# Storing two output tiles side by side in four strips, in a batched bilinear kernel on one Trainium2 core

## The reference

```python
bilinear = jnp.einsum('bie,ied->bid', feature, weight)   # feature (512, 200, 64), weight (200, 64, 64)
out = jnp.einsum('bid,bjd->bij', bilinear, feature)      # (512, 200, 200)
```

## Time and profile before

| | |
|---|---|
| median of 3 runs | 312.74 us (312.12 to 316.39) |
| profiled execution | 311.45 us |
| its span | 309.7 us |
| mean granted TensorE clock in it | 0.944 of 2.4 GHz |
| busy, share of the span: TensorE / DVE / ACT | 77% / 49% / 42% |
| TensorE's instructions | 6,784 matmuls and as many weight loads |
| DMA queue q1, share of the 16 engines' span | 91.0% |

### The profile page before, as it was taken

How to read it: one execution, slowest core, us unless ns; L and a number is a source line. 1 busy time by engine, 2 the same in 40 slices (tenths; PEclk the granted TensorE clock), 3 DMA queues, 4 the chain that set the end, 5 groups by cost and what they waited for, 6 DMA issues and landing times.

```text
span 309.7 us, 14622 instructions
## 1 busy us (share of the span) xinstructions
PE 239.8 (77%) x6784; PEld 209.1 (68%) x6784; DVE 152.7 (49%) x180; ACT 130.2 (42%) x181; POOL 12.5 (4%) x23
## 2 busy tenths in 40 slices
PE   0269757999867776899988597989975985999960
PEld 0257746878766665677977496867975975978840
DVE  0253543457654544537756443536653464736650
ACT  1343524346344433345555333344543453544530
POOL 2005700000000000000000000000000000000000
PEclk9996999899999979999999977999998799999995
DMA  7997999859999999968999999997899998577996
GB/s 259 402 421 302 366 395 380 349 218 365 359 400 404 408 414 409 413 245 351 336 415 396 412 418 413 414 392 276 336 354 400 384 418 360 229 310 295 400 410 287
DMA packets 26140, 112.35 MB, mean 363 GB/s; under 512 B 4320, under 2 KB 4320, under 8 KB 25824
## 3 DMA queue, kind: packets, MB, share of 16 engines
q1 hardware_dynamic: 26080, 111.43, 91.0%
HBM read 29.49 MB, written 81.92 MB: 360 GB/s over the span
## 4 chain that ended last, share of the span: by engine, by line
PE 77%; issue 14%; DMA 3%; SPq 1%; DVE 1%; ACT 1%
PE psum L292 50%; PE psum L263 18%; PE psum L309 8%; DMA w_sb<-w_dram 3%; SPq L152 1%; PE psum L275 1%; DVE tile L324 1%; ACT mixed L345 0%; ACT w_sb L359 0%
## 5 line engine op out<-in xcount | busy, mean ns | idle before, releaser
L292 PE MATMUL psum<-x_sb,mixed 64*64 64x200 f32 x3072 | 170.3, 354 | 27.8 <-issue 26.5
L292 PEld LDWEIGHTS psum<-x_sb,mixed 64*64 64x64 f32 x3072 | 134.3, 140 | 47.3 <-issue 35.0
L324 DVE COPY tile<-psum 128x800 f32<-128x800 f32 x100 | 99.2, 992 | 109.7 <-PE psum L292 99.2
L324 ACT COPY tile<-psum 128x800 f32<-128x800 f32 x100 | 82.5, 826 | 86.0 <-PE psum L292 69.4
L263 PE MATMUL psum<-x_sb,w_sb 64*64 64x64 f32 x3072 | 67.9, 230 | 29.9 <-issue 16.2
L263 PEld LDWEIGHTS psum<-x_sb,w_sb 64*64 64x64 f32 x3072 | 66.3, 143 | 31.0 <-issue 29.3
L345 ACT COPY mixed<-psum 64x512 f32<-64x512 f32 x48 | 27.8, 580 | 34.5 <-PE psum L263 33.9
L345 DVE COPY mixed<-psum 64x512 f32<-64x512 f32 x48 | 33.1, 689 | 10.7 <-PE psum L263 9.4
L347 ACT COPY mixed<-psum 128x512 f32<-128x512 f32 x24 | 14.1, 586 | 36.6 <-PE psum L263 36.6
L309 PE MATMUL psum<-x_sb,tails 128*32 128x200 f32 x512 | 25.3, 342 | 1.4 <-issue 1.4
L309 PEld LDWEIGHTS psum<-x_sb,tails 128*32 128x32 f32 x512 | 17.0, 108 | 8.9 <-issue 4.2
(11 more groups left out here) (3 smaller groups left out, 0.3 us busy)
## 6 DMA issues: line engine op xcount, KB each, us to landing
out_dram<-tile SPq DMA_DIRECT2D x192, 400.0 KB, 5.6
x_sb<-x_dram SPq DMA_DIRECT2D x64, 400.0 KB, 7.4
out_tail_dram<-tile SPq DMA_DIRECT2D x8, 400.0 KB, 3.6
w_sb<-w_dram SPq DMA_DIRECT2D x1, 1152.0 KB, 16.7
w_sb<-w_dram SPq DMA_DIRECT2D x4, 256.0 KB, 8.2
w_sb<-w_dram SPq DMA_DIRECT2D x1, 1024.0 KB, 14.5
```

The lines of the kernel that those rows point to most:

```text
L292: last = nc.tensor.matmul(psum[half_rows(pair), n % BANK_PAIRS * 2 + h, a * FIELDS:(a + 1) * FIELDS], mixed[half_rows(h), (CHUNKS * g + c) ...
L324: copy(tile[:, k % SLOTS, engine], psum[:, bank:bank + 2, 0:2 * FIELDS]).then_inc(copied[engine], 1)
```

## The change

Two tiles in sequence (k even, and k + 1) share one slot: they lie side by side in each partition, 12,800 bytes. There are three such slots, `tile` has the same size. SP waits for the copies of both tiles and then stores the pair in four strips, each of every fourth partition (32 packets of 12,800 bytes), and issues the loads that belong to either tile after these. The last pair is stored tile by tile in two strips each. The copies wait for the stores of the pair three places before. The output tensor holds pairs, and the tail's tiles are in it with the others; the host takes them apart.

```diff
--- before.py
+++ after.py
@@ -33,9 +33,11 @@
 
 LAST_WAITED = MIX_AFTER[(PART - CHUNK) // MIX_FIELDS]
 TAIL_AFTER = (2, 4)
-SLOTS = 6
-
-STRIPS = 2
+
+
+SIDE = 2
+SLOTS = 3
+STRIPS = 4
 STRIP_STORES = STRIPS * 16
 
 
@@ -120,9 +122,16 @@
 
 COPIES, READERS, NUMBER, OUT_TILES = count_copies()
 TILE_OF = {tile: k for k, tile in enumerate(OUT_TILES)}
-
-
-def build(nc, x, weight, out, out_tail):
+PAIRS = len(OUT_TILES) // SIDE
+
+
+def tile_copies(tile, e):
+
+    kind, g, *rest = tile
+    return COPIES[NUMBER[(kind, g, *rest, e)]][e]
+
+
+def build(nc, x, weight, out):
     sb = lambda name, shape: nc.alloc_sbuf_tensor(name, shape, F32)
 
     w_sb = sb("w_sb", [128, 2, W_OWN, EMB])
@@ -131,7 +140,7 @@
 
 
     tails = sb("tails", [128, QUADS, 2 * TAIL_TILE // (2 * TAIL), HALVES, TAIL])
-    tile = sb("tile", [128, SLOTS, 2, HALVES, 2 * FIELDS])
+    tile = sb("tile", [128, SLOTS, SIDE, 2, HALVES, 2 * FIELDS])
     psum = nc.alloc_psum_tensor("psum", [128, 2 * BANK_PAIRS, BANK], F32)
 
     sem = nc.alloc_semaphore
@@ -171,23 +180,34 @@
                 load_part1(sp, 0, p)
             for n in range(MIX_UNITS, len(W_CUTS) - 1):
                 load_w(n)
-            for k, (kind, g, *rest) in enumerate(OUT_TILES):
-                to = out_tail[g] if kind == "tail" else out[g, rest[0], rest[1]]
-                for e in range(2):
-                    n = NUMBER[("tail", g, e) if kind == "tail" else ("score", g, *rest, e)]
-                    sp.wait_ge(copied[e], COPIES[n][e])
-                for i in range(STRIPS):
-                    sp.dma_start(to[i::STRIPS], tile[i::STRIPS, k % SLOTS]).then_inc(slot_out[k % SLOTS], 16)
-                if kind == "score" and g + 1 < GROUPS:
-                    c, t = rest
-                    if c == 0:
-
-                        load_part0(sp, g + 1, t)
-                    if c == CHUNKS - 1:
-
-                        load_part1(sp, g + 1, t)
+            for pair in range(PAIRS):
+                tiles = OUT_TILES[pair * SIDE:(pair + 1) * SIDE]
+                if pair < PAIRS - 1:
+                    for e in range(2):
+                        sp.wait_ge(copied[e], max(tile_copies(tiles[0], e), tile_copies(tiles[1], e)))
+                    for i in range(STRIPS):
+                        sp.dma_start(out[pair, i::STRIPS], tile[i::STRIPS, pair % SLOTS]).then_inc(
+                            slot_out[pair % SLOTS], 16)
+                else:
+
+                    for side in range(SIDE):
+                        for e in range(2):
+                            sp.wait_ge(copied[e], tile_copies(tiles[side], e))
+                        for i in range(STRIPS // SIDE):
+                            strip = slice(i, None, STRIPS // SIDE)
+                            sp.dma_start(out[pair, strip, side], tile[strip, pair % SLOTS, side]).then_inc(
+                                slot_out[pair % SLOTS], 16)
+                for kind, g, *rest in tiles:
+                    if kind == "score" and g + 1 < GROUPS:
+                        c, t = rest
+                        if c == 0:
+
+                            load_part0(sp, g + 1, t)
+                        if c == CHUNKS - 1:
+
+                            load_part1(sp, g + 1, t)
             for s in range(SLOTS):
-                sp.wait_ge(slot_out[s], STRIP_STORES * len(range(s, len(OUT_TILES), SLOTS)))
+                sp.wait_ge(slot_out[s], STRIP_STORES * len(range(s, PAIRS, SLOTS)))
 
         @block.gpsimd
         def _(pool):
@@ -318,10 +338,11 @@
         def copies(eng, copy, engine):
 
             def copy_tile(n, k):
-                if k >= SLOTS:
-                    eng.wait_ge(slot_out[k % SLOTS], STRIP_STORES * (k // SLOTS))
+                pair, side = divmod(k, SIDE)
+                if pair >= SLOTS:
+                    eng.wait_ge(slot_out[pair % SLOTS], STRIP_STORES * (pair // SLOTS))
                 bank = n % BANK_PAIRS * 2
-                copy(tile[:, k % SLOTS, engine], psum[:, bank:bank + 2, 0:2 * FIELDS]).then_inc(copied[engine], 1)
+                copy(tile[:, pair % SLOTS, side, engine], psum[:, bank:bank + 2, 0:2 * FIELDS]).then_inc(copied[engine], 1)
 
             def score(n, g, c, t, u):
                 if u == engine:
@@ -387,17 +408,19 @@
     nc = bacc.Bacc("TRN2", target_bir_lowering=False, num_devices=1)
     args = [nc.dram_tensor("x_dram", x.shape, F32, kind="ExternalInput").ap(),
             nc.dram_tensor("w_dram", w.shape, F32, kind="ExternalInput").ap()]
-    shapes = {"out_dram": (GROUPS, CHUNKS, TILES, 128, 2, HALVES, 2 * FIELDS),
-              "out_tail_dram": (GROUPS, 128, 2, HALVES, 2 * FIELDS)}
-    args += [nc.dram_tensor(n, s, F32, kind="ExternalOutput").ap() for n, s in shapes.items()]
+    shape = (PAIRS, 128, SIDE, 2, HALVES, 2 * FIELDS)
+    args.append(nc.dram_tensor("out_dram", shape, F32, kind="ExternalOutput").ap())
     build(nc, *args)
     r = run_bass_kernel_spmd(nc, [{"x_dram": x, "w_dram": w}], core_ids=[0]).results[0]
 
-
-    rows = r["out_dram"].reshape(GROUPS, CHUNKS, TILES, 2, CHUNK, 2, HALVES, 2, FIELDS)
+    tiles = r["out_dram"].reshape(PAIRS, 128, SIDE, 2, HALVES, 2 * FIELDS).swapaxes(1, 2).reshape(
+        len(OUT_TILES), 128, 2, HALVES, 2 * FIELDS)
+    order = [TILE_OF["score", g, c, t] for g in range(GROUPS) for c in range(CHUNKS) for t in range(TILES)]
+
+    rows = tiles[order].reshape(GROUPS, CHUNKS, TILES, 2, CHUNK, 2, HALVES, 2, FIELDS)
     rows = rows.transpose(0, 6, 2, 5, 7, 3, 1, 4, 8).reshape(GROUPS, HALVES, HALF_SAMPLES, TAIL_FIRST, FIELDS)
 
-    tail = r["out_tail_dram"].reshape(GROUPS, 4, 2, HALVES, TAIL, 2, 2, 2, FIELDS)
+    tail = tiles[[TILE_OF["tail", g] for g in range(GROUPS)]].reshape(GROUPS, 4, 2, HALVES, TAIL, 2, 2, 2, FIELDS)
     tail = tail.transpose(0, 3, 5, 6, 7, 1, 2, 4, 8).reshape(GROUPS, HALVES, HALF_SAMPLES, TAIL, FIELDS)
     whole = np.concatenate([rows, tail], axis=3)
```

## The result

| | before | after |
|---|---|---|
| median | 313.03 us (312.12 to 316.39, 4 runs) | 317.12 us (316.74 to 317.93, 4 runs) |
| profiled execution's span | 309.7 us | 315.0 us |
| DMA packets on q1 | 26,080 | 19,808 |
| q1's share of 16 engines' span | 91.0% | 89.0% |

The ratio is 1.0136 (95% interval 1.0081 to 1.0191): slower by 1.4%, clear of noise. The forecast was 310.7 us, 2.0 us less than before, in a range of 305 to 317. The ratios here leave out executions that lie more than 1.5% above the fastest of the same kernel, so they may differ from the quotient of the medians, which are of all executions.

What follows compares the result with a forecast made beforehand. The prediction took DMA to bound the kernel in 195 us and TensorE in 81 us. Fewer packets saved 2.0 us, all other terms were zero: 312.74 - 2.0 = 310.7 us, range 305 to 317.

Steps and rivals of the forecast that it cites:

- bounds of 306.5 and 319 us: Limits used for the prediction's chances: 0.12 below 306.5 us, 0.80 within, 0.08 above 319 us.
- The bound: Whole span: DMA bounds the kernel in five stretches, 195 us, and TensorE in those between, 81 us.
- under 0.95: Sign of a wrong forecast: DMA share under 0.95 in 80:125 or 160:200, pointing to held tile or slots.
- the wait for `out_dram` at every other tile: Sign of a wrong forecast, pointing to the slots: ACT or DVE waiting for `out_dram` at every other tile.
- Fewer packets, -2.0 us: Stores in DMA-bound stretches: 70 tiles x 4 packets x 7 ns saved, 2.0 us; 0 to 6.2 us at the bounds.
- nothing: Rival for the stores: cost goes by bytes, or packets are cut on the way; 312.7 us, chance 0.17.
- Waiting for the second tile, 0: Five places where DMA goes from idle to busy, and DMA-bound stretches: the first tile's later store costs zero.
- comes out of that backlog: DMA-bound stretches: transfers lag the copies, so a hold of one tile (2 to 3 us) doesn't run DMA dry.
- The slots, 0: Three slots of two: five tiles take 10 us, copy to landing under 9.8 us, so it just fits; zero.
- Loads later, 0: Even tiles' loads issued one tile (3 us) later, needed well after: zero, bound 3 us once in a group.
- held tile: Rival: at five places DMA starts one store later, not absorbed, 8.7 us more; 321 us, chance 0.11.
- fetch: Rival: TensorE's instruction blocks wait 0.25 us more behind longer packets, 17 blocks, 4.2 us; 314.9 us, chance 0.06.

Runs made afterwards that it cites:

- hold_only: Kernel before with SP's new order alone (waits for both tiles, four stores, then their loads), six slots, 6,400-byte packets: 317.75 us, ratio 1.0116.
- hold_again: The same kernel as hold_only, run again in a later group: 318.70 us, ratio 1.0131.
- packets_only: Kernel before, each tile stored as copied but in 12,800-byte packets, with the loaded weights as the stores' source: 314.45 us, ratio 1.0040.
- packets_control: As packets_only, from the same weights, but in 64 packets of 6,400 bytes: 314.35 us, ratio 1.0054 to the kernel before.
- hold_first: Kernel before with the hold of hold_only in the first pair alone: 311.30 us, ratio 0.9973.
- hold_middle: Kernel before with the hold of hold_only in the pairs of chunk 1 and the tail alone: 313.06 us, ratio 1.0011.
- hold_outer: Kernel before with the hold of hold_only in the pairs of chunks 0 and 2 alone, last pair spared: 314.62 us, ratio 1.0165.
- slots_only: Kernel before, stored tile by tile in 6,400-byte packets, but a copy waits for both tiles of a pair of slots: 312.79 us, ratio 1.0040.
- loads_late: Kernel before, every tile stored at once, but an even tile's load issued after the odd tile's store: 316.95 us, ratio 1.0103 (0.9853 to 1.0353).
- hold_loads_between: hold_only with the loads at their old places, each after its own tile's stores: 315.80 us, ratio 1.0133 to the kernel before.
- hold_slots7: hold_only with seven slots instead of six, room taken from `tails` (cut to 4 groups): 316.64 us, ratio 1.0212 to the kernel before.
- lag_one: Kernel before, but SP holds every tile until the next one is copied and issues one tile at a time: 313.44 us, ratio 1.0065.

## Why the prediction was wrong

The forecast was 2.0 us less; the measured time is 1.4%, some 4 us, more. Two terms put at zero, the wait for the second tile and the slots, were the loss, and the one gain didn't show. (The chances in the prediction are worked out for bounds of 306.5 and 319 us, not for those of its range, 305 and 317; 317.12 lies between the two upper ones.)

**The bound** held: DMA in the stretches with loads, TensorE between. In the changed kernel the DMA share is 1.00 in 80:125 and 1.01 in 160:200, so the sign "under 0.95" didn't come, nor the wait for `out_dram` at every other tile (8 waits in 200 copies).

**Fewer packets, -2.0 us.** The price of a packet was of the right size in the trace's own terms: q1's busy time fell by 1.4 us (2.0 forecast), two short packets against a long one differ by 12.0 ns (7 taken). What no run bears out is the next step, that busy time saved is time won. packets_only against packets_control: 0.14%, and in the traces 410 against 411 and 407 against 410 GB/s. The fits of the earlier trace rows measured the durations of packets, which overlap (shares above 1.0 in the earlier trace rows show as much); the rate would have been the thing to compare, and it is 408 to 422 GB/s for 6,400 bytes. The rival "nothing" described this part. These two runs agree with the Trainium skill's line rate from 512 B on (DMA: Bandwidth & Descriptors, Specifications): no gain from 6,400 to 12,800 B can be measured.

**Waiting for the second tile, 0.** This is the step that failed and decided: hold_only and hold_again measure +1.2% and +1.3%, 3.6 to 4.1 us. I had priced the places where the engines go from idle to busy, and no run shows these to be wrong: no cost of the first pair (hold_first) nor, by the ratios, of chunk 1 (hold_middle, within 0.5%). What I waved through with "comes out of that backlog" is what costs: the hold in the DMA-bound chunks (hold_outer, +1.65%). What the step left out may be that a backlog, which keeps the engines busy, is also what TensorE's instructions queue behind: in the kernel before the packet for the next block starts 2.7 to 3.8 us into the block under full engines, and within 0.5 us at the best where they aren't full. I had priced the backlog as cover alone and the fetch as a rival of long packets alone. That the hold costs by this way is not shown; how it costs stays open.

**The slots, 0.** +0.4% (slots_only), 1.3 us by the ratio, which hardly excludes zero. "It just fits" was no reason for zero: the margin worked out there was 10 us against 9.8.

**Loads later, 0.** Not settled: loads_late's interval holds everything from a gain to a loss of 3%. hold_loads_between shows only that the loss doesn't need it.

**The sum** after the fact: 1.2 + 0.4 - 0.1 = 1.5% by single parts, 1.36% measured together. Each part is known to half a per cent or so, so the sum shows that no large part is missing, and no more. The rival "held tile" had the right part and the wrong places: it priced five starts at 2 to 2.65 us each, 8.7 us in all. The rival "fetch" had TensorE's instructions wait longer because packets are longer; packets_only, with 49.3 us of waits on "issue" against 48.7 in its control, shows no such delay.

**What stays open** is how the hold costs in chunks 0 and 2. Late stores alone don't explain it: the lag holds twice as many tiles at half the price. Slots alone don't: with seven no copy waits for one, and the kernel with the hold still takes 2.1% more than before. Four stores and two loads issued at once, with TensorE's instructions behind them, fit hold_slots7 and lag_one. But at six slots hold and lag aren't apart beyond their intervals, the waits on "issue" over the whole span are much the same with and without the hold, the one stretch followed above has no load in it, and no run removed the fetch while it kept the burst. Nor does a trace of hold_outer show the loss: its profiled execution took 311.63 us, as long as the median of before.

## What to carry to other kernels

Before storing two things together to make longer packets, compare the rates in GB/s at both packet sizes, not the packets' durations: those overlap, and the time saved on them can be nothing. A stored item that waits for its neighbour can cost where the DMA engines are full, where a backlog seems to cover it, and not only where they idle; here it did, for a reason that is still open. Price a hold, a slot less and a packet size by a run each; here the three parts add up to the whole, as far as their intervals tell. And before a wait in one stretch of a trace is called the cause, look at the same stretch in a second trace of the same kernel: here they lay 3.4 us apart.

## What the runs showed that was not expected

Packets of 12,800 bytes take 495.4 ns and two of 6,400 take 2 x 253.7 ns in the trace, with 410 and 411 GB/s moved. A busy share of the DMA engines is thus no measure of their rate within 2% in these windows. One more slot brought nothing (0.9962, 0.9892 to 1.0032) though one fewer with a hold costs a per cent more. Single executions of the unchanged kernel in these groups ran from 306.7 to 322.2 us, far wider than the 312.1 to 316.4 of its first three; even 6 to 12 executions of each kernel, with the kernel before beside them, leave intervals of half a per cent and more, and in loads_late one of 2.5% each way.
